# A graph network's edge layer written out as 168 steps in place of seven iterations of 24, with counting spread over its steps and edge records loaded in a ring

## The reference

```python
for l in range(6):
    W = ssp(edge_attr @ mlp_w1[l] + mlp_b1[l]) @ mlp_w2[l] + mlp_b2[l]
    W = W * C[:, None]                       # C: cosine cutoff of the edge length
    msg = (h @ conv_w1[l])[src] * W
    agg = segment_sum(msg, dst, num_segments=2500)
    h = h + (ssp(agg @ conv_w2[l] + conv_b2[l]) @ lin_w[l] + lin_b[l])
x = layernorm(x + h)
for l in range(3):
    z = (1.0 + eps[l]) * h + segment_sum(h[src], dst, num_segments=2500)
    h = relu(z @ W1[l] + b1[l]) @ W2[l] + b2[l]
x = layernorm(x + h)
```

## Time and profile before

| | |
|---|---|
| median of three runs | 4573.64 us (4567.78 to 4575.24) |
| span of the profiled execution | 6617.0 us |
| mean granted TensorE clock in it | 0.778 of full speed |
| PE, DVE, ACT, POOL busy in it | 72%, 46%, 33%, 45% |
| gathers in it | 2982 |

### The profile page before, as it was taken

How to read it: one execution, slowest core, us unless ns; L and a number is a source line. 1 busy time by engine, 2 the same in 40 slices (tenths; PEclk the granted TensorE clock), 3 DMA queues, 4 the chain that set the end, 5 groups by cost and what they waited for, 6 DMA issues and landing times.

```text
span 6617.0 us, 88816 instructions
## 1 busy us (share of the span) xinstructions
PE 4785.2 (72%) x24401; PEld 3558.4 (54%) x24684; DVE 3028.4 (46%) x8117; ACT 2174.5 (33%) x3585; POOL 2995.9 (45%) x3161
## 2 busy tenths in 40 slices
PE   0376777867777777777777777767777777777789
PEld 0365555645555555555555555545555555555544
DVE  3244444544444444444444444544444444444532
ACT  0133333333333333333333333333333333333322
POOL 5634444444454445444445444444445444445400
PEclk5687777777777777777777777777778777777799
DMA  4452233233233333233333323233333332323300
GB/s 157 137 151 84 83 86 88 82 91 85 82 87 85 85 90 89 80 86 86 86 86 91 85 84 88 85 85 87 85 85 88 86 89 84 86 84 87 87 14 9
DMA packets 324938, 574.64 MB, mean 87 GB/s; under 512 B 73578, under 2 KB 117300, under 8 KB 322996
## 3 DMA queue, kind: packets, MB, share of 16 engines
q1 hardware_dynamic: 202572, 357.07, 17.9%
q0 software_dynamic: 100160, 203.51, 11.5%
q10 hardware_dynamic: 21928, 11.64, 0.6%
HBM read 524.00 MB, written 47.93 MB: 86 GB/s over the span
## 4 chain that ended last, share of the span: by engine, by line
PE 40%; another core or an unknown queue 27%; issue 13%; DVE 10%; DVEq 4%; ACT 4%; POOL 2%; DMA 1%; ACTq 0%; SPq 0%; POOLq 0%
PE ps_w L680 10%; PE ps_h L781 9%; PE ps_a L695 8%; PE ps_a L692 4%; PE ps_pair L894 3%; POOL permuted L551 2%; DVE ex_msg L1428 2%; PE ps_pair L707 2%; DVEq L342 2%; ACT ps_w L1025 1%; DVE aggT L1409 1%; PE ps_a L669 1%; DVE phot L1388 1%; ACT xc L1062 1%
## 5 line engine op out<-in xcount | busy, mean ns | idle before, releaser
L561 POOL DMA_INDIRECT rows<-node_table,src_all x2982 | 2820.5, 946 | 3117.5 <-DVE ex_msg L1428 1937.8
L680 PEld LDWEIGHTS ps_w<-edge_w,hid 128*128 128x128 f32 x8064 | 1336.7, 242 | 1295.6 <-issue 1295.3
L680 PE MATMUL ps_w<-edge_w,hid 128*128 128x128 f32 x8064 | 1392.8, 329 | 719.0 <-ACT ps_w L1025 471.4
L1571 DVE SCALAR_TENSOR_TENSOR hid<-xc,ps_h 128x512 f32<-128x512 f32 x1008 | 690.9, 686 | 1859.5 <-remote 1328.5
L1060 ACT ACTIVATE xc<-ps_h 128x512 f32<-128x512 f32 x1008 | 601.3, 597 | 2648.2 <-remote 1363.6
L781 PE MATMUL ps_h<-buffers,edge_w 112*128 112x512 f32 x2016 | 1347.9, 756 | 86.4 <-DVE hid L1571 46.3
L695 PE MATMUL ps_a<-hot,ex_msg 128*128 128x32 f32 x6048 | 952.1, 306 | 469.7 <-issue 251.2
L695 PEld LDWEIGHTS ps_a<-hot,ex_msg 128*128 128x128 f32 x6048 | 887.8, 226 | 522.6 <-issue 512.8
L1062 ACT ACTIVATE xc<-xc,half_col 128x512 f32<-128x512 f32 x1008 | 727.3, 722 | 32.6
L1025 ACT COPY ps_w<-seed_rows 128x512 f32<-128x512 f32 x1008 | 591.6, 587 | 413.9 <-DVE ex_msg L1428 342.8
L1416 DVE TENSOR_TENSOR aggT<-aggT,ps_a 128x32 f32 x756 | 140.4, 186 | 927.2 <-remote 631.0
(11 more groups left out here) (236 smaller groups left out, 2825.5 us busy)
## 6 DMA issues: line engine op xcount, KB each, us to landing
buffers<-in_attr SPq DMA_DIRECT2D x756, 224.0 KB
buffers<-src_select SPq DMA_DIRECT2D x252, 256.0 KB
buffers<-attr_permuted SPq DMA_DIRECT2D x252, 224.0 KB
rows<-node_table,src_all POOLq DMA_INDIRECT x2982
permuted<-aggT SPq DMA_DIRECT2D x7, 1248.0 KB, 17.6
hid<-permuted SPq DMA_DIRECT2D x42, 208.0 KB
counts<-in_rec SPq DMA_DIRECT2D x4, 1924.0 KB, 35.4
hi_mid<-node_table SPq DMA_DIRECT2D x6, 1280.0 KB
```

The lines of the kernel that those rows point to most:

```text
L561: pool.indirect_dma_start(out=rows[:, use % RS, t * F:(t + 1) * F], out_offset=None, in_=table[:, :], in_offset=bass.IndirectOffsetOnAxis( ...
L680: mm = pe.matmul(ps_w[u % 2][:, t * F:(t + 1) * F], hid[:, u % 2, t * P:(t + 1) * P], edge_w[:, EW_W2:EW_W2 + F], start=False, stop=(t == ...
L1571: dve.scalar_tensor_tensor(out=hid[:, i % 2, :], in0=xc[:, i % 2, :], scalar=LOG_MAX, in1=ps_h[i % 2][:, :], op0=ALU.min, op1=ALU.max).the ...
```

## The change

A layer becomes one straight program of 168 steps on every engine (`U = 168`); the loop over iterations, its `If(it > 0)` parts, `iteration_slices` and the four sliced copies are gone, and tiles are read from `rel`, `cut`, `prel`, `pcut` in place. A layer now has 108 count tiles in 27 groups, each at a step of its own: `count_steps()` gives steps 4 to 145, apart from 58 to 62 and 102 to 106 nearly all that are no multiple of four. Early chunks start at steps 60, 104 and 148 (before: 72, 120, 144) and wait for the counts issued before them. The tables of starts share one tensor, in four quadrants of 32 partitions. `rec` holds two quarters; the load of quarter c waits for the scatter of quarter c - 2. Ranks go in chunks of two blocks, ten in place of seven.

```diff
-U = 24
+U = 168
-NIT = 7
-NP_GROUPS = NIT * J
-NQ_GROUPS = NIT * J * (M - 1)
+NP_GROUPS = J
+NQ_GROUPS = J * (M - 1)
-BG = -(-REAL // (L0 * NIT))
+BG = -(-REAL // L0)
-CLEARS, REC_LOADS = 7, 4
+CLEARS, REC_LOADS, REC_RING = 7, 4, 2
-PRIME = 2
-EARLY_AT = [3, 5, 6]
+PRIME = 4
+EARLY_STEP = [60, 104, 148]
-RANK_BLOCKS = 3
+RANK_BLOCKS = 2
-COUNT_STEP = [4, 4, 5, 6, 8, 9, 10, 11, 13, 13, 14, 15, 17, 18, 19, 20]
+COUNT_STEP = count_steps()
+assert len(COUNT_STEP) == len(set(COUNT_STEP)) == BT
...
             for c in range(REC_LOADS):
-                part = slice(c * RT // REC_LOADS, (c + 1) * RT // REC_LOADS)
-                sp.dma_start(rec[:, part, :], rec_d[:, part, :]).then_inc(rec_in[c], 16)
-            sp.wait_ge(scattered, RT * 16)
+                first, end = REC_STARTS[c], REC_STARTS[c + 1]
+                if c >= REC_RING:
+                    wait_scattered(sp, c - REC_RING)
+                sp.dma_start(rec[:, c % REC_RING, 0:end - first, :], rec_d[:, first:end, :]).then_inc(rec_in[c], 16)
+            for c in range(REC_LOADS - REC_RING, REC_LOADS):
+                wait_scattered(sp, c)
...
-                    for it in range(NIT):
-                        uses = Uses(pool, layer * (K * NIT) + k * NIT + it)
...
+                        for use in range(first, last):
+                            uses.wait(msg_done, group_of(use - RS))
+                            pool.sem_inc(gate, 1)
+                            gather_group(use, use, table_d[half])
...
-                    with pe.Fori(0, NIT) as it:
-                        uses = Uses(pe, layer * (K * NIT) + k * NIT + it).ready(-1, -5)
-                        early_step = load_early(pe, it)
-                        for i in range(U):
...
+                    uses = Uses(pe, layer * K + k).ready(-1, -5)
+                    for i in range(U):
+                        if i in EARLY_STEP:
+                            early_step = load_early(pe, EARLY_STEP.index(i))
...
+                        if i >= 4:
+                            aggregate(uses, i - 4)
+                        if i in EARLY_STEP:
+                            with pe.If(early_step > 0):
+                                early = load_early(pe, EARLY_STEP.index(i), 1)
+                                pe.wait_ge(node_w_in, layer * 16 + 16)
+                                uses.wait(add_done, i - 1 - ADD_LAG)
+                                uses.wait_count(count_added, counted_until(i) - 1)
+                                chunk_prod1(pe.snap(early * CH - CH), layer * NCH + early)
...
-                        dve.tensor_scalar(phot[:, t, :], pwin_now[:, :], prel_now[:, first + t:first + t + 1],
-                                          pcut_now[:, first + t:first + t + 1], ALU.is_equal, ALU.mult)
+                        dve.tensor_scalar(phot[:, t, :], pwin_now[:, :], prel[:, first + t:first + t + 1],
+                                          pcut[:, first + t:first + t + 1], ALU.is_equal, ALU.mult)
...
-                                window_ready(layer * K + k)
-                                uses.wait(msg_done, -1)
-                                iteration_slices(it, n)
-                                count_slices_now(counted, n)
+                        if i == 2:
+                            window_ready(layer * K + k)
+                            count_slices_now(counted, n)
```

More of the change, by code:

```diff
@@ L54 @@
 EACH = -(-E // P)
-CLEARS, REC_LOADS = 7, 4
-REC_STARTS = [c * RT // REC_LOADS for c in range(REC_LOADS)]
+CLEARS, REC_LOADS, REC_RING = 7, 4, 2
+REC_STARTS = [c * RT // REC_LOADS for c in range(REC_LOADS + 1)]
+REC_MAX = -(-RT // REC_LOADS)
 CLEAR_PARTS = 16
@@ L93, with count_steps, group_of, added_before @@
 GW_W1, GW_W2, GW_B1, GW_B2, GW_EPS, GW_N = 0, F, 2 * F, 2 * F + 1, 2 * F + 2, 2 * F + 3
-COUNT_STEP = [4, 4, 5, 6, 8, 9, 10, 11, 13, 13, 14, 15, 17, 18, 19, 20]
-assert len(COUNT_STEP) == BT
+def count_steps():
+    bounds, steps = [1] + EARLY_STEP + [U], []
+    room = [(end - first - 6) // 4 * 4 for first, end in zip(bounds, bounds[1:])][:EARLY]
+    wanted = [4 * round(BG * n / sum(room)) for n in room]
+    wanted[0] += BT - sum(wanted)
+    for first, end, n in zip(bounds, bounds[1:], wanted):
+        free = range(first + 3, end - 2)
+        light = [i for i in free if i % M]
+        heavy = [i for i in free if not i % M]
+        extra = n - len(light)
+        if extra > 0:
+            light += [heavy[j * len(heavy) // extra] for j in range(extra)]
+        else:
+            light = [light[j * len(light) // n] for j in range(n)]
+        steps += sorted(light)
+    return steps
+COUNT_STEP = count_steps()
+assert len(COUNT_STEP) == len(set(COUNT_STEP)) == BT
 def use_of(u):
     return u // M * (M - 1) + u % M - 1
+def group_of(use):
+    return use // (M - 1) * M + use % (M - 1) + 1
+def added_before(step):
+    return sum(not permuted(u) for u in range(step - ADD_LAG))
 def gathers_of(g):
@@ L162, in gnn_program @@
         base_f = sb("base_f", [P, NG])
[L163 to L166, removed]
+        starts = sb("starts", [P, PAD + PT], i32)
+        pbase_i, block_i, base_i, pbase_kept = (starts[32 * i:32 * (i + 1), :] for i in range(4))
+        base_i, pbase_kept = base_i[:, 0:LEAD + NG], pbase_kept[:, 0:PT].bitcast(f32)
         prel = sb("prel", [P, PT])
@@ L1071, in _ @@
-                    uses = Uses(act, layer * (K * NIT) + k * NIT + (NIT - 1))
+                    uses = Uses(act, layer * K + k)
+                    uses.ready(-1, -5)
+                    for u in range(U):
+                        if u in EARLY_STEP:
+                            early_step = load_early(act, EARLY_STEP.index(u))
+                        if u - 1 in EARLY_STEP:
+                            with act.If(early_step > 0):
+                                chunk_softplus(layer * NCH + load_early(act, EARLY_STEP.index(u - 1), 1))
+                        if u - 3 in EARLY_STEP:
+                            with act.If(early_step > 0):
+                                early = load_early(act, EARLY_STEP.index(u - 3), 1)
+                                chunk_store(act.snap(early - 1), layer * NCH + early, next_half)
+                        uses.wait(mm1_done, u)
+                        act.activation(xc[:, u % 2, :], ps_h[u % 2][:, :], ACT.Exp).then_inc(exp_done, 1)
+                        uses.wait_step(exp_done, u)
+                        act.activation(xc[:, u % 2, :], xc[:, u % 2, :], ACT.Ln, bias=half_col[:, :]
+                                       ).then_inc(log_done[u % M], 1)
+                        if u >= 2 and permuted(u - 2):
+                            keep_picked(uses, u - 2)
+                        if u >= 1:
+                            seed(uses, u - 1)
@@ L1072, in _ @@
+                    uses = Uses(act, layer * K + k)
                     seed(uses, U - 1)
-                with act.If(load_early(act, NIT - 1) > 0):
+                with act.If(load_early(act, EARLY - 1) > 0):
                     late_chunks(layer, EARLY, next_half)
```

378 lines of the change are left out of this document (160 added, 218 removed).

## The result

The kernel after takes **4713.81 us** (median of 4 runs, 4704.07 to 4723.59), the kernel before 4574.44 (4567.78 to 4575.52): ratio 1.0307, 95% interval 1.0291 to 1.0323. It is 3.1% slower where I had forecast 0.7% faster, and lies outside the range of 4450 to 4625.

A forecast was written before the change was run, and what follows sets the result against it. Two level chains were taken to bound a layer, gathers at 626.5 us and PE-DVE steps at 628. Gathers summed to 4533 to 4550, ranks +1, with 4 to 7 us a layer of lag gone: 4542 us, range 4515 to 4562.

The forecast's parts named there:

- (e): Waits in a layer: chunk products wait for counts added one step earlier, the gather's wait is unchanged; cost 0.
- (c): Count tiles: 108 a layer for 112, sitting singly, mostly on steps without select products; saves 3 us a layer.
- Chain 2: PE and DVE working by steps: 628 us a layer before the change, 586 after.
- (a) to (c): PE-DVE steps: jumps back gone 24 us, slice copies and repeated count operations 15, fewer tiles 3; 42 a layer.
- The gather chain: GpSimd issuing 497 gathers a layer at 1.247 us pitch: 626.5 us, then 2.3 and 20.3 to the next layer.
- rival A: Nothing to take: the timed run already follows the gathers alone; about 4570 us, chance 0.17.
- (f): PE's instructions, loaded anew each layer in 34 q8 packets without idle time: 0; ACT's code at most 9 us.
- rival C: PE starves for code, each q8 packet exposing a gap; 4623 us at 1.58 each, 5112 at 4.0; chance 0.15.
- (g): Setup: two-quarter record ring covered by 9 us, DVE's delayed work still in time; ranks in smaller chunks add 1 us.
- (d): Early chunks moved to steps 60, 104, 148: amounts unchanged, a late one has 20 steps to be made up.
- (h): Cold jump back of the layer loop on PE or ACT: 4 us, hidden behind the gather ring's 30 us.
- Rival B: Gathers not the limit in timed runs, their spacing being shorter unprofiled; 4321 us, or up to 4500; chance 0.12.

The follow-up runs named there:

- f2: The kernel before, unchanged, run again for a trace on a chip where it takes 4574 us; 4590.82 us.
- e1b: Kernel after with its 108 count tiles in groups of four steps, one free step between groups; 4569.09 us, ratio 0.9996 to before.
- e6: The e1b kernel with 413 gathers a layer in place of 497; 4355.48 us, ratio 0.9522 to before.
- e3b: Kernel before, loops kept, with count tiles at steps 4 to 19, so three groups an iteration begin right behind the last; 5137.74 us, ratio 1.1234.
- e4: Kernel after with all four quarters of the records held at once, on chip 12; 6594.87 us, ratio 0.9959 to before.
- e7: Kernel after with 413 gathers a layer in place of 497, on chip 10; 6002.64 us, ratio 0.9077 to before.
- f1: Kernel after with 413 gathers a layer in place of 497, where before takes 4574 us; 4717.04 us, ratio 1.0314 to before.
- f3: The e1b kernel with every third group permuted instead of every fourth, 441 gathers a layer for 497; 4493.25 us, ratio 0.9819 to before.

## Why the prediction was wrong, point by point

- **The step that failed is (e)**, with the sentence on tiles in (c). I priced the chunk products' wait for counts and the gather's wait, both rightly at 0, and I wrote that tiles "sit singly, mostly on steps without select products". I did not ask what a single tile a step does to the one wait that count tiles have among themselves, PE's first tile of a group on DVE's addition of the last. The wait is in code the diff hardly touches (count_tile, add_counts). The old list kept the groups a step apart; the new function doesn't. The method of the prediction, to name for each moved step what is queued behind it, would have found it had I written out the first nine of the new steps: 4, 5, 6, 7, then 9, 10, 11, 13, then 14: the second group ends at 13 and the third begins at 14. Price: 60.6 us a layer in the steps' chain, which then takes 646 us for the 586 forecast and no longer fits under the 626.5 of the gathers.
- **Chain 2 was right but for this.** Forecast 628 before and 586 after without a new wait; measured 621 and 585. Jumps, slices and fewer tiles together are worth 36 us a layer where (a) to (c) said 42, and 29 once the start of a layer is counted in.
- **The gather chain was right in its terms and short at the layer's end.** 626.5 us a layer: measured 626 to 628. The gap from last gather to the next layer's first was 2.3 + 20.3 = 22.6 in the sum, and is 25 to 27 (once 30) in the traces: over four gaps 15 us more, in f2 and in e1b alike, of the 23 to 40 that the sum lacked. I had put 4 to 7 us a layer down to steps that lag behind the gathers, and to be won. The last message does come 7.2 us or more behind the last gather in f2 and not 2.3, but in e1b, whose steps have some 40 us to spare, it still comes 5.4 to 7.7 behind: it is the emptying of the pipeline, which the change doesn't shorten. That is the term behind the 0.7% gain I forecast: it wasn't there. Without the wait the change is worth 0 (0.9997 and 0.9996). So rival A, "nothing to take", told the size rightly, at 4570 against 4569 and 4574, for the kernel that the change would have been; the point I held against it, the chunks of iterations 5 and 6, did not decide.
- **(f) and rival C.** q8 has 224 packets, 37 a layer for the 34 worked out, and PE doesn't idle at them: e6's steps run at 585 us on the streamed code, and in its second layer PE's waits called issue come to 0.6 us. The slowing came from the side C stands on, but its mechanism was absent. The Trainium skill ("Runtime: NRT & Kernel Launch", Instruction fetch mechanics), by which the crossings in sequential code are mostly hidden, agrees with PE's trace inside a layer. POOL's gathers show 7 to 10 us of excess a layer in f2 and in e1b, as taken from the row.
- **(g)** right: the ring is covered, setup 1 to 2 us shorter, not 1 longer. **(d)**: no cost seen; the longest step behind each of the three chunks lasts the same in after and in e6 (6.73, 7.06 and 7.17 us in the mean of layers 2 to 6). **(h)** was off for the kernel as it ran: PE idles 4.5 to 5.0 us at the start of a layer, by its place the cold jump back. Where the gathers set the pace it is hidden, as I reckoned (e1b takes no longer than before). Where the steps do, as in after, it shows: the way from one layer's steps to the next is 5 to 6 us longer.
- **Rival B** is out: the pitch of the gathers is 1.25 us in f2 and e1b too.
- **The pauses** The earlier trace rows were rightly kept out of the sum, for a wrong reason: they go with the chip and not with the profiling, since on chips 10 and 12 every timed run of before takes over 6590 us. So the forecast that a profile of after would stay near 6500 was wrong (4709.9).

## What to carry to other kernels

When work that fills a single buffer is spread more thinly over a software pipeline, count the steps from the last use of one filling to the first of the next, on both engines, and where in each engine's step they stand; an average load per step says nothing of it. The mend is one free step between groups, or the draining instruction at the head of its step. And before crediting a saving, find the chain that sets the pace by lightening it (here fewer gathers: -0.7% before, -4.7% with the steps relieved, 0 with the waits): two chains that are level to 1% give nothing when only one is shortened.

## What the runs showed of the hardware

- A wait of PE of 2.4 to 2.8 us costs 3.6 (after) to 4.8 us (e3b). In the timeline shown the granted clock fell to its lower level some 2 us after PE had begun again and stayed there some 3.4 us. The mean clock follows: 0.937 in e1b, 0.925 in after, 0.887 in e3b. An estimate from the means: at two levels, 0.925 over 4709.9 us is 706 us at the lower one, 0.950 over 4357.5 (e6) is 436, so each of the 102 waits brings 2.7 us at half speed and loses 1.3 by it; 3.6 less 2.37 is 1.2.
- Written out, PE's code of a layer streams with hardly any idle time (0.6 us in e6's second layer), but at the start of each layer PE idles 4.5 to 5.0 us (after, layers 2 to 6), where the kernel with short loops has no idle time (f2).
- The same kernel takes 4574 us on some chips and 6618 on others, and did so in every run on the two (6591 to 6650). There the signals of PE reach ACT and DVE late, as in the earlier trace rows, while GpSimd's pitch of 1.247 and the last stage, which has no gathers, are as elsewhere. Time there goes with the number of gathers even where the steps set the pace: from e4 to e7 504 gathers fewer gave 592 us, 1.2 us each (the ring of the records, and chip 10 for 12, aside), where from after to f1 the same 504 gave nothing. What delays the signals stays open; it wasn't tried by itself.
- A permuted group costs the steps little more than a gathered one (3 to 5 us for 14), though PE does eight products more in it. In the second layer PE was busy, as the profile models it, 560.4 of 585 us in e6 and 570.5 of 590 in f3: half of the added work went into its idle time. With 3 to 4% of idle left, PE's own work is nearly the whole of a step in both.
